# Attention groups with the scores behind V and all turns in one stretch; the experts' turns in other banks

## What is computed

```
# attention in windows of 8x8 tokens, 8 heads of 8 channels
qkv = xw @ qkv_w.T + qkv_b
q, k = _rope2(q), _rope2(k)
attn = softmax(q * scale @ k.T)
h = (attn @ v) @ proj_w.T + proj_b
# scan over the 4096 tokens of an image
h = h + _selective_scan(layernorm(h), delta, A, Bm, Cm, D)
# experts: the best of 32 for each token
xf  = layernorm(h)
idx = argmax(xf @ router_w.T + router_b)
out = relu(relu(xf @ W1[idx] + b1[idx]) @ W2[idx] + b2[idx])
h = h + out
```

## Time and profile before

| | us |
|---|---|
| median of 3 runs | 604.15 (603.57 to 606.45) |
| the profiled execution | 605.85 |
| its span | 604.1 |
| TensorE busy | 542.7 (90%) |
| VectorE busy | 491.1 (81%) |
| ScalarE busy | 403.3 (67%) |
| GpSimd busy | 350.0 (58%) |

### The profile page before, as it was taken

The page is one execution under the profiler, slowest core; times in us unless marked ns, Lnnn a source line. Parts: engine busy times, 40 slices in busy tenths (PEclk is TensorE's granted clock), DMA queues, the critical chain, the costliest instruction groups (busy, mean ns, idle before and its releaser), DMA issues. The chain is left out here.

```text
span 604.1 us, 18372 instructions
## 1 busy us (share of the span) xinstructions
PE 542.7 (90%) x7273; PEld 389.6 (65%) x7274; DVE 491.1 (81%) x910; ACT 403.3 (67%) x723; POOL 350.0 (58%) x388
## 2 busy tenths in 40 slices
PE   5897999999999999999657757579999999999996
PEld 4897889998989989997212223345555555555553
DVE  3888788888888888886799999768888878788873
ACT  3676788888888888888697576124545455454543
POOL 8306377777777777774898598553333343333320
PEclk9899999999999999999788798869999999999999
DMA  9732222222222222210000000000101101010111
GB/s 193 113 51 47 63 60 55 62 58 63 61 55 61 60 57 63 58 35 3 1 0 0 0 1 1 3 2 18 26 22 23 24 20 26 20 26 20 26 23 27
DMA packets 62382, 23.06 MB, mean 38 GB/s; under 512 B 45780, under 2 KB 62292, under 8 KB 62292
## 3 DMA queue, kind: packets, MB, share of 16 engines
q1 hardware_dynamic: 61200, 21.63, 17.6%
q10 hardware_dynamic: 964, 0.20, 0.2%
q0 software_dynamic: 128, 0.00, 0.0%
HBM read 5.02 MB, written 4.19 MB: 15 GB/s over the span
## 5 line engine op out<-in xcount | busy, mean ns | idle before, releaser
L772 DVE TENSOR_REDUCE work<-psum 128x16 f32<-128x1024 f32 x64 | 78.1, 1220 | 29.4 <-PE psum L604 29.4
L707 ACT ACTIVATE work<-work 128x1024 f32<-128x1024 f32 x64 | 67.8, 1060 | 21.6 <-DVE work L777 21.6
L777 DVE TENSOR_TENSOR work<-psum,work 128x1024 f32<-128x1024 f32 x64 | 78.4, 1225 | 2.2
L715 ACT ACTIVATE work<-psum 128x512 f32<-128x512 f32 x128 | 70.9, 620 | 2.4 <-PE psum L619 1.5
L619 PE MATMUL psum<-kc,work 128*128 128x128 f32 x512 | 67.6, 275 | 4.3 <-ACT work L707 3.5
L1687 POOL TENSOR_TENSOR m_rstd<-m_var,m_mhalf 128x4 f32<-128x4 f32 x32 | 32.2, 1008 | 61.8 <-DVE m_var L1897 61.8
L1798 ACT ACTIVATE hid<-psum,b1c 128x512 f32<-128x512 f32 x96 | 58.9, 684 | 13.2 <-PE psum L1702 13.2
L635 PEld LDWEIGHTS psum<-work 128*64 128x64 f32 x2048 | 62.3, 138 | 5.3 <-issue 5.3
L635 PE MATMUL psum<-work 128*64 128x18 f32 x2048 | 65.5, 212 | 0.0
L619 PEld LDWEIGHTS psum<-kc,work 128*128 128x128 f32 x512 | 58.8, 141 | 8.8 <-ACT work L707 4.5
L1710 PE MATMUL psum<-x_t,w1x 64*64 64x256 f32 x1024 | 64.4, 391 | 0.0
(11 more groups left out here) (198 smaller groups left out, 1285.2 us busy)
## 6 DMA issues: line engine op xcount, KB each, us to landing
work<-big_bc SPq DMA_DIRECT2D x256, 32.0 KB, 2.0
h_all<-in_x SPq DMA_DIRECT2D x16, 256.0 KB, 5.3
work<-big_a SPq DMA_DIRECT2D x32, 128.0 KB, 2.2
out<-out_st SPq DMA_DIRECT2D x126, 32.0 KB
w1x<-in_L_ffn_W SPq DMA_DIRECT2D x2, 128.0 KB, 3.6
kc<-constants SPq DMA_DIRECT2D x1, 202.0 KB, 2.9
w2x<-in_L_ffn_W SPq DMA_DIRECT2D x1, 128.0 KB, 3.3
work<-in_L_tok_qkv_w ACTq DMA_DIRECT2D x2, 32.0 KB, 3.3
```

What stands on the lines that cost most here:

```text
L707: act.activation(prob[:, f], prob[:, f], ACT.Exp).then_inc(prob_done, 1)
L715: act.activation(prob_t[:, f, 4 * half:4 * half + 4, :].rearrange("p j q -> p (j q)"), banks[4 + half][:, :], ACT.Copy).then_inc(prob_t_do ...
L772: dve.tensor_reduce(top[:, f, :].rearrange("p (g h) -> p g h", g=4), sc, AX.X, ALU.max).then_inc(top_done, 1)
L777: dve.tensor_tensor(prob[:, f].rearrange("p (g h) k -> p g h k", g=4), sc, top[:, f, :].rearrange("p (g h) -> p g h", g=4).unsqueeze(3).br ...
```

## The change

In attention, TensorE's body is put in another order. `scores(i + 2)` stands at the end of `body(i)`, behind `values(i + 1)`, where it was `scores(i + 1)` at the start. Both turns of quad i, `turn_o(i - 1)`, `turn_u(i - 4)` and `project(i - 1)` stand in one stretch before the products. The array is then full for one stretch, works on 64 columns for the products and V, and on 32 rows for the scores. For the first quad, `scores(1)` is put behind `turn(0, 0)`. ScalarE's and GpSimd's bodies follow: `copy_v` goes behind the exponentials of the second half, the masks of q and k in front of the bias and the square. In the experts, the turned marks of the first pair go to bank 1 (beside x) and y has bank 2 alone; y is turned before x, and x now waits for the copy of the marks, which y did before.

```
--- before.py
+++ after.py
@@ run_pool
             if live(i, 3):
...
+            if live(i, -2) and i >= -1:
+                pool.wait_ge(qk_staged[par], (i + 2) // 2 * 128 + 128)
+                pool.wait_ge(scores_done, i * 4 + 8)
+                mask_qk(pool, t, i + 2)
             if live(i, 2):
...
-            if live(i, -2) and i >= -1:
-                pool.wait_ge(qk_staged[par], (i + 2) // 2 * 128 + 128)
-                pool.wait_ge(scores_done, i * 4 + 8)
-                mask_qk(pool, t, i + 2)
@@ run_pe
         def body(i, par):
-            if live(i, -1):
-                scores(i + 1)
+            if live(i, 0):
+                turn(i, 0)
+                if first(i):
+                    scores(1)
+            if live(i, 1):
+                turn_o(i - 1)
             if live(i, 4):
                 turn_u(i - 4, i)
             if live(i, 0):
                 turn(i, 1)
             if live(i, 1):
-                turn_o(i - 1)
+                project(i - 1)
             if live(i, 0):
                 products(i, par, 0)
                 products(i, par, 1)
             if live(i, -1):
                 values(i + 1)
-            if live(i, 1):
-                project(i - 1)
-            if live(i, -1):
-                turn(i + 1, 0)
+            if live(i, -2) and i != -1:
+                scores(i + 2)
@@ run_act
         def body(i, par):
+            if live(i, 0):
+                copy_t(i, 0)
+            if live(i, 1):
+                copy_o(i - 1)
...
             if live(i, 0):
                 copy_t(i, 1)
-            if live(i, 1):
-                copy_o(i - 1)
             amid(i)
             if live(i, -1):
                 exps(i + 1, 0)
-                copy_v(i + 1, 1 - par)
-                exps(i + 1, 1)
-                copy_t(i + 1, 0)
             if live(i, 1):
                 act.wait_ge(proj_done, i)
...
+            if live(i, -1):
+                exps(i + 1, 1)
+                copy_v(i + 1, 1 - par)
@@ experts, TensorE
                     pe.wait_ge(chosen, i - 1)
-                    pe.wait_ge(h_done, min(i + 1, QUADS))
+                    pe.wait_ge(lg_done, i - 1)
...
-                            m = pe.matmul(psum[0:96, (2, 6)[b], 256 * b + k * P:256 * b + k * P + P],
+                            m = pe.matmul(psum[0:96, (1, 6)[b], 256 + k * P:256 + k * P + P],
...
-                if live(i, 1):
-
-                    pe.wait_ge(xh_done, i)
-                    if not first(i, 1):
-                        pe.wait_ge(lg_done, i - 1)
-                    for n in range(2):
-                        m = pe.transpose(psum[:, 1, n * P:n * P + P], xh[:, 2 * n:2 * n + 2, :], ident)
-                    m.then_inc(x_turned, 1)
                 if live(i, -1):
                     pe.wait_ge(y_staged, i + 2)
                     if not first(i, -1):
                         pe.wait_ge(h_done, i + 1)
+                    for n in range(2):
+                        m = pe.transpose(psum[:, 2, n * P:n * P + P], y_st[:, n, :], ident)
+                    m.then_inc(y_turned, 1)
+                if live(i, 1):
+
+                    pe.wait_ge(xh_done, i)
                     if live(i, 2):
                         pe.wait_ge(mark_act, i - 1)
                     for n in range(2):
-                        m = pe.transpose(psum[:, 2, 256 + n * P:256 + n * P + P], y_st[:, n, :], ident)
-                    m.then_inc(y_turned, 1)
+                        m = pe.transpose(psum[:, 1, n * P:n * P + P], xh[:, 2 * n:2 * n + 2, :], ident)
+                    m.then_inc(x_turned, 1)
```

More of the change, by code:

```diff
@@ L1807, in body @@
                     act.wait_ge(mark_turned, i * 2 - 3)
-                    act.activation(mark_t[:, 0, :], psum[0:96, 2, 0:256], ACT.Copy).then_inc(mark_act, 1)
+                    act.activation(mark_t[:, 0, :], psum[0:96, 1, 256:512], ACT.Copy).then_inc(mark_act, 1)
                 if live(i, 1):
@@ L1858, in body @@
                     dve.wait_ge(y_turned, i + 2)
-                    dve.tensor_tensor(h, h, psum[:, 2, 256:512].rearrange("p (s d) -> p s d", s=4), ALU.add
+                    dve.tensor_tensor(h, h, psum[:, 2, 0:256].rearrange("p (s d) -> p s d", s=4), ALU.add
                                       ).then_inc(h_done, 1)
```

## The result

| | us |
|---|---|
| kernel before, median of 20 runs | 605.63 (603.48 to 606.84) |
| changed kernel, median of 20 runs | 606.93 (604.52 to 608.8) |
| ratio, 95% interval | 1.0026 (1.0014 to 1.0037) |
| profiled execution of the changed kernel | 604.52, of which 602.8 span |

The change costs 0.26%, some 1.6 us (0.8 to 2.2), which is less than the 0.5% that counts as no change here. The medians themselves differ by 1.3 us. The forecast's difference was +1.2 us.

What follows compares the result with a forecast made beforehand. TensorE's own sum was taken as attention's period, 6.98 us a quad. Start +4.0, quads -2.0, end -0.8 and experts 0 gave +1.2 us; scaled to the median of runs, 605.4 us, range 601.0 to 608.8.

Steps and rivals of the forecast that it cites:

- One change of the array gone of four, three left: Attention, TensorE: V to scores still costs a full change; a quad's work falls from 6.98 to 6.79 us, some 0.195 less.
- the rival by which this step is free: Attention: the step from 64 columns to 32 rows costs nothing, a quad takes 6.7 us, the whole 599.6; chance 0.10.
- The wait for ScalarE's copies: Attention, second half's turn: waits 0.07 us for the bank's copy, its second four 0.05 more; a quad gains 0.075.
- The long reaction: Attention: TensorE goes on 0.15 us after ScalarE's copy ends, not 0.05; the wait is 0.12 us instead of 0.02.
- the quad of 6.81: Attention rival: TensorE sees ScalarE's copies 0.05 us after their end, a quad takes 6.81, the whole 602.6; chance 0.20.
- The start: Attention's first quads: V's later copies delay scores(1) and scores(2) by 2.33 us, quad 1's products by 4.0, once.
- rival 4: Start of attention: TensorE waits longer and works at half speed for longer, up to 2.3 us more, 607.7 or above; chance 0.05.
- The way back: Attention from quad 3 on: some 27 quads give back 0.075 us each, 2.0 us in all.
- The end: End of attention: quad 30's projection stands before the last products, so 0.8 of VectorE's 0.99 us idle before its delta returns.
- Rival 3: Experts: logits wait for the later copy of x, 0.10 us a quad, 3.1 us in all, 608.5; chance 0.18.
- TensorE's row stays: Experts: the marks' copy holds whichever turn stands last, so x takes y's place; cost 0.
- GpSimd's masks at nothing: Attention, GpSimd: masks stand earlier and have the products' time to be ready; cost nothing, cover the spare 0.7 us.

Runs made afterwards that it cites:

- `proj_back`: Changed kernel with the projection again behind V and ScalarE's copies of it behind V's, four array changes a quad: 611.96 us, ratio 1.0114.
- `u_behind`: Changed kernel with u turned and copied behind the second half's turn instead of before it: 618.13 us, ratio 1.0213 to the kernel before.
- `late_proj`: Changed kernel with the projection one quad later, between u and the second half's turn, and output behind that turn: 610.12 us, ratio 1.0071.
- `v_first`: Changed kernel, but for quad 0 ScalarE copies V right behind the first exponential, as before: 604.38 us, ratio 0.998 to the kernel before.
- `exp_only`: Kernel before with only the experts changed, attention as before: 606.1 us, ratio 1.001.

## Why the prediction was right, point by point

**The sum.** Forecast 1.2 us of difference, measured 1.6 (0.8 to 2.2). The absolute 605.4 is 1.5 below the 606.93 measured. The kernel before, measured again beside it, also stands 1.5 higher than the median of three that the forecast was scaled to, so that the scale was off by as much. That the difference came out so well is in part luck: the traces give attention +0.3 us of the +1.2 forecast, the experts +0.4 where nothing was forecast, and what makes up the rest isn't located.

**One change of the array gone of four, three left.** Right. The earlier trace rows were read a little too high: their 0.20 has in it 0.11 which such a product takes anyway (from 52.21 to 52.32), so leaving costs 0.1 there, and what entering costs the scores is in their 1.10 before and after. The sum took V's 0.60 unchanged and isn't touched by this. V's step to the scores takes 0.59, as V's step to the projection did in the earlier trace rows, and the rival by which this step is free fell. `proj_back` paid 0.24 for a fourth change, by the forecast's terms 0.20 and 0.04 of waiting, for the copy of u.

**The wait for ScalarE's copies.** Right in place and in kind, a little too large: 0.07 before the second half, as worked out. The 0.05 before its second four did not come; there are 0.03 behind its first transpose instead, which the forecast didn't have. So 6.88 instead of 6.91. The long reaction that was chosen from the earlier trace rows held before the second half, and the quad of 6.81 did not come. `u_behind` moved the wait by what the formula gives. The forecast looked at the banks of the two halves alone; `u_behind`, `proj_back` and `late_proj` ran into banks 6 and 7 next.

**The start.** 2.33 and 2.33 for the scores, as forecast; 3.91 for the products of quad 1 instead of 4.0. The mechanism of rival 4 came in its first half and cost nothing: TensorE did work at the lower clock for longer (0.50 against 0.63 from 57 to 61 us), but under waits. Before `scores(2)` the clock was back at 1.00 and stayed there. `v_first` shows that it needn't: with the scores 2.36 earlier TensorE slowed down at this place and lost 1.27 of that.

**The way back.** From the products of quad 1 to those of quad 31 the distance shrank by 3.91 - 1.36 = 2.5 us, 0.10 a quad, with one quad 0.11 longer; forecast 2.0.

**The end.** 1.06 came back between the last products and the first delta, where I took 0.8 of 0.99. VectorE's delta starts with no idle time at all, so all of the wait and a little of the work in front of it went; `proj_back`, with the projection behind the products again, has a wait of 1.02 there. Attention with the scan's start is thus +0.3 in the trace, and not +1.2: the two terms that give back were each undersized, by 0.5 and by 0.3, and the start was oversized by 0.1.

**Experts.** Right in the steady quad: y and x change places, and the logits stand 0.06 behind the copy of x. Rival 3 did not come. The step that failed is "TensorE's row stays": it stays only while y is there. In the last two quads there is no y, x now waits where nothing did, and 0.4 us is lost. And "a gain is excluded" was true of this change, but the wait it named was worth 0.2 us a quad to whoever took it away by choosing banks otherwise.

**GpSimd's masks at nothing.** Right for this change, but the cover was much thinner than the "spare 0.7 us" of busy time suggests. `u_behind` moved one turn of 0.22 us behind a block of 0.90, and the masks' 0.97 us of room were gone down to 0.10; VectorE then waited 0.90 a quad for GpSimd.

**What stays open.** The traces account for 0.5 us of a difference measured as 0.8 to 2.2. The rest may lie in the spread of stage 1 (2.3 us) and of the scan's length (`exp_only`'s was 1.4 us longer than before's with nothing changed there), or in a clock that falls more often than in the execution that was profiled: the mean granted clock of the changed kernel's 20 runs is 0.957, where its profiled one has 0.959 and 29 runs of the kernel before have 0.963. No trace here settles it. The long quads of `u_behind` and `late_proj` aren't explained either.

## What to carry to other kernels

When blocks are regrouped to save changes of the array, count the changes from the rows of the timeline, and then work out, for each pair of blocks that share a bank, what cover is left between them: here one half of the saving went to that. Do it for every bank, for the next order can be held by another one, as in `late_proj`. An order that is better in the steady state should be started in the old way where its first round isn't covered yet, and the last rounds, in which one block is missing, need a look of their own. A wait that stands in every round is worth more than the order around it: another bank for the marks gave 5.7 us in the medians, the whole regrouping without its start 2.7 in the trace up to the first delta.

## What the hardware showed that I had not expected

- TensorE fell to 1.2 GHz in the middle of attention behind a wait of 1.67 us (`v_first`; busy for 0.71 of 2 us, then clock 0.81 and 0.62 in two stretches of 3 us). It did not behind one of 1.45 us at the same place in the changed kernel, where it had been busy for 1.71 of those 2 us. Each is one execution. Work that starts earlier can so lose most of what it gained.
- TensorE's reaction to the end of another engine's instruction took several values: 0.05 us in the start (58.86 behind V's copies, which ended at 58.81), 0.10 in `late_proj` (163.66 behind 163.56) and behind GpSimd's masks in `u_behind` (163.18 behind 163.08), and 0.14 in the experts' quads (414.27 behind 414.13), in attention's (159.25 behind 159.11) and in `u_behind` (167.93 behind 167.79). What decides between them isn't known.
- Leaving a shape of the array cost 0.1 us wherever it was read: output before the products, 0.31 instead of 0.22; the last product of the earlier trace rows, 0.20 instead of 0.11; the projection before the scores in `proj_back`. Entering the full array cost 0.10 from 64 columns (the projection) and 0.06 from 32 rows (the first half, 0.93 instead of 0.87).
- Behind a wait, the first transpose of a block was followed by the next after 0.14 us instead of 0.11 (the second half in the changed kernel, output in `late_proj`).
